# Attention reordered from whole batches to a chunk pipeline, with K and V projected in hi/lo parts and the output projection in plain fp32

## The reference, cut to what matters

```python
h = layernorm(x)
Q, K, V = h @ Wq.T + bq, ctx @ Wk.T + bk, ctx @ Wv.T + bv      # per batch 512 x 512
scores = Q_h @ K_h.T / sqrt(32)                                # per head 512 x 512
x = x + concat_h(softmax(scores) @ V_h) @ Wo.T + bo
y = layernorm(x)
w = top-2 of softmax(y @ Wr.T + br)                            # per token, 8 experts
x = x + sum_e w_e * down_e((up_e(y) + 1) * glu(gate_e(y)))
```

## Time and profile before

| what | value |
| --- | --- |
| profiled execution | 1896.04 us, of it span 1894.3 us |
| median of three runs | 1895.62 us |
| attention, first projection to last logits | 22.9 to 1092.0 us |
| one batch in the steady state | 133 us |
| experts | 1141 to 1894 us |
| TensorE busy / VectorE busy, share of the span | 92% / 72% |
| mean granted TensorE clock | 0.962 |

### The profile page before, as it was taken

The page is one execution under the profiler, slowest core; times in us unless marked ns, Lnnn a source line. Parts: engine busy times, 40 slices in busy tenths (PEclk is TensorE's granted clock), DMA queues, the critical chain, the costliest instruction groups (busy, mean ns, idle before and its releaser), DMA issues. The chain is left out here.

```text
span 1894.3 us, 31367 instructions
## 1 busy us (share of the span) xinstructions
PE 1735.4 (92%) x10597; PEld 1253.6 (66%) x10597; DVE 1366.4 (72%) x2488; ACT 667.7 (35%) x1107; POOL 469.7 (25%) x628
## 2 busy tenths in 40 slices
PE   5989989989989999899899827999999999999996
PEld 4537547447356365375474427998989889889895
DVE  3775775775766757757757587778787888888874
ACT  2252342441532622523524404233434343434221
POOL 3212113013022032121122002343333333334332
PEclk9999999999999999999999958999999999999998
DMA  6404306206117025044052042253636535636322
GB/s 220 127 2 135 111 1 169 77 25 171 52 44 202 2 76 170 2 119 127 1 141 62 36 145 80 69 218 101 227 92 224 201 124 191 216 123 230 92 79 78
DMA packets 103797, 216.06 MB, mean 114 GB/s; under 512 B 25936, under 2 KB 26960, under 8 KB 103632
## 3 DMA queue, kind: packets, MB, share of 16 engines
q1 hardware_dynamic: 75696, 135.27, 22.4%
q0 software_dynamic: 27936, 78.73, 13.2%
HBM read 204.19 MB, written 37.36 MB: 128 GB/s over the span
## 5 line engine op out<-in xcount | busy, mean ns | idle before, releaser
L1265 PE MATMUL gu_ps<-xgT_hi,wg_hi 128*128 128x256 f32 x1248 | 354.9, 284 | 0.0
L1265 PE MATMUL gu_ps<-xgT_hi,wg_lo 128*128 128x256 f32 x1248 | 351.7, 282 | 0.0
L1265 PE MATMUL gu_ps<-xgT_lo,wg_hi 128*128 128x256 f32 x1248 | 351.5, 282 | 0.0
L448 ACT ACTIVATE pt<-st 128x1024 f32<-128x1024 f32 x256 | 249.4, 1018 | 152.2 <-PE st L291 152.2
L1265 PEld LDWEIGHTS gu_ps<-xgT_hi,wg_hi 128*128 128x128 f32 x1248 | 235.5, 189 | 0.0
L1265 PEld LDWEIGHTS gu_ps<-xgT_lo,wg_hi 128*128 128x128 f32 x1248 | 235.5, 189 | 0.0
L1265 PEld LDWEIGHTS gu_ps<-xgT_hi,wg_lo 128*128 128x128 f32 x1248 | 235.3, 189 | 0.0
L609 DVE TENSOR_REDUCE negmax<-work 128x1 f32<-128x512 f32 x256 | 175.0, 689 | 62.4 <-PE work L276 61.3
L1325 ACT ACTIVATE sig<-gate 128x256 f32<-128x256 f32 x156 | 65.0, 417 | 303.1 <-DVE gate L1377 303.1
L291 PE MATMUL st<-qs,ks 98*128 98x512 f32 x512 | 165.1, 416 | 5.8 <-ACT pt L448 5.1
L609 DVE TENSOR_REDUCE negmax<-st 128x2 f32<-128x1024 f32 x128 | 151.6, 1218 | 25.6 <-PE st L276 23.9
(11 more groups left out here) (195 smaller groups left out, 3170.5 us busy)
## 6 DMA issues: line engine op xcount, KB each, us to landing
raw_g<-w_gate_up SPq DMA_DIRECT2D x39, 2048.0 KB
raw_d<-w_down SPq DMA_DIRECT2D x39, 1024.0 KB
ks<-k_hi SPq DMA_DIRECT2D x256, 64.0 KB, 2.1
qs<-q_hi SPq DMA_DIRECT2D x256, 64.0 KB, 2.5
bd<-b_down SPq DMA_DIRECT2D x39, 256.0 KB
x_in<-x SPq DMA_DIRECT2D x8, 1024.0 KB, 5.3
ctxT<-ctx_t SPq DMA_DIRECT2D x8, 1024.0 KB, 5.7
ks<-k_lo POOLq DMA_DIRECT2D x128, 64.0 KB, 2.4
```

What stands on the lines that cost most here:

```text
L448: e.activation(pt[k % 2][:, 2 * p:2 * p + 2, :], st[st_ring.bank[b, "exp", c, k, p]][:, :, :], ACT.Exp, scale=scale).then_inc(exped.sem, 1)
L1265: ins = e.matmul(gu_ps[n % GU_BANKS][:, part, :], wg[s][pw][:, k, cols], xgT[s][px][:, k, :], start=(k == 0 and m == 0), stop=(k == KD - 1 ...
```

## The change

The stage gets one list, ORDER, built from steps; each engine walks the same list and does its own part of each entry. A unit u is one chunk of one batch (32 units). Step s weighs unit s, takes the maxima of unit s + 1 and projects a third, unit s + 2, also across the border of a batch. K uses three passes (fp32r) on a split ctx and a split wk. V uses three passes too, with half the features (256 columns) of two token blocks in a unit. The output projection uses one plain float32 matmul where it used three passes, so o_hi and o_lo go; so do the two further copies of hi and lo tiles (one hi and one lo tile now serve K and Q in turn). qs and ks become rings of three. All maxima use the small work buffers, one block at a time; st serves only the exponentials. Input loads, residual adds, ln2, turns of x, logits and stores are entries of the list and go by token block.

```diff
+        def step(s):
+            b, c = divmod(s, C)
+            main, early, late = [], [], []
+            if s in units:
+                for k in range(T):
+                    ahead = (s, k + 1) if k + 1 < T else (s + 1, 0)
+                    if ahead[0] in units:
+                        main += [("exp", *ahead, p) for p in range(2)]
+                    main += [("weigh", s, k), ("sum", s, k)]
+            if c == 3 and b in bs:
+                early += [("residual", b)]
+            if s + 1 in units:
+                early += [("max", s + 1, h, t) for h, t in ROWS] + [("turn_max", s + 1)]
...
+            if s + 2 in units:
+                u = s + 2
+                to, i = divmod(u, C)
+                if i == 0:
...
+                    late += [("ctx", to, k) for k in range(C)]
+                    late += [("turn_x", to, t) for t in range(T)]
...
+                late += spread(norm[:2], [("k", u, k) for k in range(C)])
+                vs = [("v", u, j, k) for j in range(2) for k in range(C)]
+                late += vs[:3] + [("low", u, "k")] + spread(norm[2:], vs[3:])
+                if i == C - 1 and to + 1 in bs:
+                    late += [("load_ctx", to + 1)]
+                late += [("q", u, k) for k in range(C)]
+                late.insert(-2, ("v_out", u))
...
+            after = []
+            if c == 0 and b - 1 in bs:
+                after += [("out", b - 1, t, k) for t in range(T) for k in range(C)]
+            if c in (1, 2) and b - 1 in bs:
+                after += [("turn_xln", b - 1, 2 * (c - 1) + j) for j in range(2)]
+            if c == 3 and b + 2 in bs:
+                after += [("stats", b + 2), ("ln1", b + 2)]
+            if s + 2 in units:
+                after.insert(min(1, len(after)), ("low", s + 2, "q"))
+            first = 10
...
+            keys = spread(main[:first], early) + spread(main[first:], late + after)
...
+            def row_max(u, h, t):
+                to, i = take(work_ring, "max", u, h, t), u % RING
+                if (h, t) == ROWS[0]:
+                    e.wait_ge(k_stacked.sem, k_stacked[u])
+                    e.wait_ge(k_stacked_lo.sem, k_stacked_lo[u])
+                    e.wait_ge(q_stacked.sem, q_stacked[u])
+                    e.wait_ge(q_stacked_lo.sem, q_stacked_lo[u])
...
+            def qk_hi(n, u):
+                e.wait_ge(projected.sem, projected[u, n])
+                if n == "q":
+                    e.wait_ge(k_stacked.sem, k_stacked[u])
+                elif u:
+                    e.wait_ge(q_stacked.sem, q_stacked[u - 1])
...
+            def stack_hi(n, u):
+                e.wait_ge(hi_made.sem, hi_made[u, n])
...
+                for part in places:
                     for r in range(GROUP):
-                        e.dma_start(dst[HD * part:HD * (part + 1), r, :].bitcast(F32),
-                                    hi[n][c % 2][HD * r:HD * (r + 1), :].bitcast(F32)).then_inc(stacked[c].sem, 16)
+                        e.dma_start(dst[u % RING][HD * part:HD * (part + 1), r, :].bitcast(F32),
+                                    hi[HD * r:HD * (r + 1), :].bitcast(F32)).then_inc(landed.sem, 16)
```

More of the change, by code:

```diff
@@ L162, in attention_stage @@
+        eps2_added, rstd2_made = Mark(sem("eps2_added"), TOKENS), Mark(sem("rstd2_made"), TOKENS)
         bo_added = Mark(sem("bo_added"), bs)
         work_uses, st_uses = [], []
[L168 to L176, removed]
-            use_st((b, "logits"), parts_made, b)
-            use_st((b, "sum"), logits_out, b)
@@ new lines, in on_pe @@
+            e.wait_ge(s_init, N_INIT)
+            for kind, *what in ORDER:
+                if kind == "exp":
+                    exp_scores(*what)
+                elif kind == "weigh":
+                    weigh_values(*what)
+                elif kind == "sum":
+                    sum_weights(*what)
+                elif kind == "max":
+                    row_max(*what)
+                elif kind == "turn_max":
+                    turn_max(*what)
+                elif kind in "kq":
+                    project(kind, *what)
+                elif kind == "v":
+                    project_v(*what)
+                elif kind == "out":
+                    project_out(*what)
+                elif kind == "turn_x":
+                    turn_x(*what)
+                elif kind == "turn_xln":
+                    turn_xln(*what)
+                elif kind == "logits":
+                    if what == [0, 0]:
+                        e.wait_ge(s_consts, N_CONSTS)
+                    route_logits(*what)
+                elif kind == "logit_sum":
+                    sum_logits(*what)
@@ L624, in o_lo @@
[L624 to L636 removed]
+                    e.wait_ge(rstd1_made.sem, rstd1_made[b])
@@ new lines, in on_dve @@
+            ln1_stats(0)
+            ln1(0)
+            for kind, *what in ORDER:
+                if kind == "max":
+                    reduce_max(*what)
+                elif kind == "turn_max":
+                    max_lo(*what)
+                elif kind == "low":
+                    if what == [0, "k"]:
+                        e.wait_ge(s_consts, N_CONSTS)
+                    qk_lo(*what)
+                elif kind == "v_out":
+                    v_out(*what)
+                elif kind == "norm":
+                    normalise(*what)
+                elif kind == "out" and what[2] == C - 1:
+                    add_residual(*what[:2])
+                elif kind == "ln2":
+                    ln2(*what)
+                elif kind == "stats":
+                    ln1_stats(*what)
+                elif kind == "ln1":
+                    ln1(*what)
+                elif kind == "split":
+                    weight_lo(*what)
+                elif kind == "ctx":
+                    ctx_lo(*what)
+                elif kind == "turn_x":
+                    x_lo(*what)
+                elif kind == "logit_sum":
+                    add_router_bias(*what)
```

1102 lines of the change are left out of this document (451 added, 651 removed).

## The result

The changed kernel takes 2156.92 us in the median of four runs (2155.97 to 2158.02); the kernel before, 1896.12 us beside it (1894.84 to 1897.66). The ratio is 1.1375, 95% interval 1.1356 to 1.1395: slower by 261 us. The prediction said 2130 us, range 2005 to 2230. The profiled execution has a span of 2154.2 us; its mean granted clock is 0.91 where it was 0.96.

The account below looks back on a forecast made before the run. TensorE, busy 92% of the span, was taken to bound the kernel. A batch of 134.4 + 20.8 (waits) + 6 (clock) = 161 us against 133 moved attention's end from 1092 to 1329: about 2133, said as 2130 us, range 2005 to 2230.

Parts of the forecast that it names:

- stacking chain: From T0, the start of Q's last matmul, through copy, DMA issues and landing: 8.1 us by the hi way.
- phase A: A step's maxima part: 14.4 us, coupled to VectorE's reductions through two buffers, 3.1 us more than TensorE's work.
- work with no new wait: A steady batch: four steps of 14.4 + 14.1 us plus 20.4 us once a batch, 134.4 us.
- waits at the first M: TensorE waits for Q's stacking at the start of a step's maxima: 4.6, 4.1 and 7.6 us in three steps.
- waits at the turning of x and at K behind it: At c = 2, splits of ctx and x share two small buffers ahead of K: 3.5 us a batch.
- half clock in phase A, three times: Half clock behind three waits a batch, 2 us each: 6 us, with bounds 0 and 8 for each.
- c = 3: Step where statistics and root precede Q's lo part and its DMAs: chain ends at T0 + 10.5, wait 7.6 us.
- rival 1: Maxima and reductions don't couple; phase A is TensorE's 12.1 us, giving 2059 us; chance 0.12.
- rival 4: Stacking is hidden and phase A is TensorE's, so a batch takes 122 us, giving 1820 us; chance 0.06.
- the filling: Start of the pipeline: first projection about 19, its three 8.4, stacking 8.1 us, and more; step 0 begins at 66.
- 2: Rival: the clock stays low through phase A, 156 us more, giving 2286 us; chance 0.10.
- 3: Rival: ln1 on VectorE delays GpSimd's lo DMA issues at c = 3, 13 us more, 2143 us; chance 0.10.

Follow-up runs that it names:

- e6: The changed kernel with the output projection as three fp32r matmuls instead of one float32 product, Wo and lo parts left out: 2132.53 us, ratio 1.1247.
- e1: The changed kernel with maxima taken from the chunk stacked one step earlier, so the first M doesn't wait for stacking (wrong maxima): 2020.2 us, ratio 1.0648.
- e3: The changed kernel with each maximum reduced over 256 of the 512 columns, so VectorE's reductions are shorter: 2100.0 us, ratio 1.1076.
- b1: The kernel before, with GpSimd's addition of bo issued ahead of the root for the next batch: 1855.2 us, ratio 0.9781.
- e2: The changed kernel with unused fp32r matmuls filling TensorE's wait at the first M of a step: 2130.61 us, ratio 1.1239.
- e5: The changed kernel with the eight hi DMAs shared by SyncE and ScalarE, and Q's lo part ahead of the statistics at c = 3: 2121.07 us.
- e4: The changed kernel with K and V projected in plain float32, without the split of ctx, wk and wv: 2158.06 us, ratio 1.1383.

## Why the prediction was right

**What it rested on.** Three claims carried the sum: the change saves TensorE next to nothing, every step gets a wait of the stacking chain's length less its cover, and phase A is paced by VectorE. All three stand: e6 and the rows for the first (K's twelve matmuls 450.44 to 453.25, 2.81 us where the sum has 2.78; V's 24 at c = 2 take 2.84 without the two E between them, for 2.86), e1 for the second, e3 for the third. By terms, for the steady batch (the measured work is the batch less the rows under it):

| term | predicted | measured |
| --- | --- | --- |
| work with no new wait | 134.4 | 133.6 |
| waits at the first M | 5.6 + 4.1 + 7.6 = 17.3 | 4.20 + 3.76 + 6.92 = 14.9 |
| waits at the turning of x and at K behind it | 3.5 | 2.30 + 0.56 = 2.9 |
| waits for the lo part of Q at the turned rows | none | 1.13 + 1.22 = 2.35 |
| half clock in phase A, three times | 6 | 2.7 + 2.4 + 1.6 = 6.7 |
| half clock behind the turning of x (an estimate) | none | 3.3 |
| batch | 161 | 163.75 |

**The chain of stacking.** T0 + 8.1 was predicted and 7.8 measured at 516.81; c = 3 was T0 + 10.5 and is 9.8, ended by the lo way as said. The 1.0 us for the load of ctx at c = 1 did not show: the wait there is 4.20, against 4.6 without it.

**Phase A.** 14.4 us with the last E; measured, at full clock, 13.64 to the turning (13.02 at c = 0) and 0.66 for the E behind it (532.82 to 533.48), 14.3. e3 takes 1.87 us off a phase by shorter reductions. The prediction gives TensorE's own pace twice, 11.3 us and, in rival 1, 12.1 with the turning and the last E; e3's 11.15 + 0.66 = 11.8 lies nearer the second, so the 122.0 us of a batch, on which rival 4 rests, were 2 to 3 us too few.

**Where it was short.** 27 us in all; 3 of them lie in saying 2130 where the sum gave 2133. The step that was mis-sized is the clock: I counted it behind three waits of a batch and forgot the fourth, the turning of x, though the prediction itself had put 3.5 us of waiting there. Behind it the clock is at 0.52 from 493 to 500 (the row above), which costs some 3.3 of the 7 us; that is an estimate, about half of the stretch, and no run took this cost away by itself. Then the token blocks turned behind Q: I used them as cover for the chain and noted that the second takes q_lo's buffer, but gave this no time; it is 2.35 us a batch. The two together are 5.6 us, and the half clock in phase A is 0.7 more; against them the waits at M and at x came out 3.0 smaller and the rest of the work 0.8. So a batch is only 2.75 us over its 161 because errors of both signs met: that much of the closeness is luck.

By stretches, taken from the first M of each: step 0 begins at 74.41 us instead of 66 (8.4 more), step 4 follows 155.1 us later instead of 157, step 28 980.5 us after that instead of 966 (14.5 more), and the last logits, at 1353.7, another 143.7 instead of 140. In the filling the very first M stands at 41.12, where the terms 19, 8.4 and 8.1 give 35.5: the first K begins at 21.68 and not at 19, the three projections up to Q's last matmul at 31.57 take 9.9 and not 8.4, the chain behind it 9.55 and not 8.1. (The terms of the filling, as written, add up to 64.5 and not 66.)

**The rivals.** 1 (phase A at TensorE's pace) fell with e3. 2 (low clock through phase A) fell with the rows of the profile: 0.59 for 10 us and 1.00 for the next 6. 4 (hidden stacking) fell with the waits; e1 shows that even without them a batch takes 147.5 to 149.4 us, so the supposed 122 would need the coupling, the turning of x and the border at c = 3 out of the way too. 3 said that ln1 on VectorE holds up GpSimd's issues at c = 3. The two do run side by side there (551.79 and 551.86), and four issues take 2.19 us instead of 1.96: 0.23 us late, not 2.2. The rule of the Trainium skill behind that rival ("SBUF — State Buffer", sections "SBUF: two separate sides" and "Who interferes with whom") would have given 13 us; this trace shows six times 0.2. Its other half, the exclusion of tensor_scalar in a two-port mode and GpSimd for a whole instruction, agrees with the rows of before: a single operation took up to 4.77 us, which is the addition's 4.53 and a bit, and in b1 all 32 take 0.54 to 0.55.

## What to carry to other kernels

In a pipeline of finer steps each border at which a stage's product is used at once costs the chain of copy, issues and landing less what the consumer has left to do, and then the clock behind it. The product should be there a whole step before its use; e1 shows what that is worth (137 us), but no run here does it with nothing left out. Cost the clock behind every wait of some microseconds, one's own new waits first. And look for the hole before rebuilding the stage: the kernel before had one of 6.1 us a batch (133 less 126.9), and moving one GpSimd addition ahead of the root for the next batch closes it.

## What the runs showed of the hardware

- The cost of the half clock did not grow with the wait: behind waits of 4.20, 3.76 and 6.92 us the next phase, which VectorE paces in part, lost 2.7, 2.4 and 1.6 us. Matmuls without use in the wait kept the clock up (1.00 in these phases of e2).
- A DMA of 64 KB within SBUF costs its issuer 0.60 to 0.62 us on SyncE, 0.70 on ScalarE and 0.49 to 0.50 on GpSimd (2.41, 2.79 and 1.96 us for four each in e5, all at once). SyncE and GpSimd are no slower for issuing beside the others; ScalarE was not seen issuing alone. For Q's pieces the landing got later beside the others on GpSimd's queue, median 2.7 us instead of 2.2, and is 3.0 on ScalarE's; on SyncE's it stayed at 2.1.
- Work taken from TensorE came back in full where nothing else had to be done for it (24 us for e6), and not at all where it needed a split on ScalarE and VectorE ahead of a wait (e4).
